# Selective-scan attention of the last layer: a new order of TensorE's work within a step, and D times u made by ScalarE

## The reference, cut to what matters

```python
u, z = jnp.split(x @ in_w.T, 2, axis=-1)
u = silu(sum(u_pad[:, k:k + L, :] * conv_w[:, k] for k in range(4)) + conv_b)
dbc = u @ xproj_w.T                                  # dt (64), B (16), C (16)
dt = softplus(dbc[..., :64] @ dt_w.T + dt_b)
dA = jnp.exp(dt[..., None] * A)
dBu = (dt * u)[..., None] * Bm[:, :, None, :]
h = dA_t * h + dBu_t ; y_t = sum_n(h * C_t)          # scan over t
y = ys.swapaxes(0, 1) + u * D
return y * silu(z) @ out_w.T
```

## Time and profile before

| | |
|---|---|
| median of 3 runs | 3783.09 us (3774.97 to 3783.92) |
| span of the profiled execution | 3806.1 us; the profile gives no other time of its own |
| stretch of the 256 scan steps | first scan 2620.0 us, last scan 3510.4 us |
| busy over the whole span | TensorE 89%, VectorE 63%, ScalarE 49%, GpSimd 45% |

### The profile page before, as it was taken

The page is one execution under the profiler, slowest core; times in us unless marked ns, Lnnn a source line. Parts: engine busy times, 40 slices in busy tenths (PEclk is TensorE's granted clock), DMA queues, the critical chain, the costliest instruction groups (busy, mean ns, idle before and its releaser), DMA issues. The chain is left out here.

```text
span 3806.1 us, 70702 instructions
## 1 busy us (share of the span) xinstructions
PE 3386.1 (89%) x24704; PEld 2274.3 (60%) x24704; DVE 2409.4 (63%) x5387; ACT 1861.9 (49%) x5051; POOL 1726.8 (45%) x1887
## 2 busy tenths in 40 slices
PE   6888888869999989999997999988999999998496
PEld 3555553547777756666663444436777777776274
DVE  3888762546666656666663444457888888888134
ACT  4666664456666635444444000036666667664033
POOL 2555541327777743333330000013676676676644
PEclk8999998989999999999998999998999999999697
DMA  4888850030000000000002777752552222222423
GB/s 132 215 210 209 210 135 11 1 76 1 2 2 2 1 1 1 2 2 1 2 1 67 159 152 152 151 101 80 122 122 71 79 78 72 79 76 65 141 69 106
DMA packets 312553, 300.58 MB, mean 79 GB/s; under 512 B 72137, under 2 KB 227721, under 8 KB 311946
## 3 DMA queue, kind: packets, MB, share of 16 engines
q1 hardware_dynamic: 307594, 286.58, 30.7%
q0 software_dynamic: 4608, 9.48, 0.8%
HBM read 237.45 MB, written 58.53 MB: 78 GB/s over the span
## 5 line engine op out<-in xcount | busy, mean ns | idle before, releaser
L2413 DVE TENSOR_TENSOR_SCAN a_h<-a_dA,a_dBu_psum 128x512 f32<-128x512 f32 x512 | 596.0, 1205 | 119.0 <-issue 106.3
L2298 POOL TENSOR_TENSOR a_h<-a_h,main_g 128x512 f32<-128x512 f32 x256 | 384.2, 1503 | 256.6 <-DVE a_h L2413 246.5
L1246 POOL TENSOR_SCALAR a_probs<-a_probs,a_row_inv 128x128 f32<-128x128 f32 (+1 forms) x512 | 381.2, 765 | 163.9 <-DVE a_row_inv L1209 163.9
L1712 DVE SCALAR_TENSOR_TENSOR m_hidden<-m_h_psum,m_gate_spread 128x512 f32<-128x512 f32 x256 | 176.9, 692 | 263.6 <-PE m_h_psum L1650 251.1
L179 POOL TENSOR_TENSOR main_g<-main_g,main_s 128x512 f32<-128x512 f32 x28 | 44.0, 1606 | 649.8 <-ACT main_g L161 649.8
L1515 POOL TENSOR_TENSOR r_position_q<-r_turned_q 128x512 f32<-128x512 f32 x128 | 160.0, 1272 | 387.3 <-DVE r_turned_q L1560 387.3
L2009 PE MATMUL a_dBu_psum<-a_B_diag,a_dt_u_turned 64*128 64x128 f32 x4096 | 317.1, 289 | 20.6 <-DVE a_h L2413 19.8
L1472 ACT ACTIVATE r_probs<-r_logits_psum,r_neg_max 128x256 f32<-128x256 f32 x512 | 235.5, 476 | 141.0 <-DVE r_neg_max L1566 141.0
L2009 PEld LDWEIGHTS a_dBu_psum<-a_B_diag,a_dt_u_turned 64*128 64x128 f32 x4096 | 257.9, 188 | 74.9 <-issue 71.0
L1151 ACT ACTIVATE a_probs<-a_logits,a_neg_max 128x128 f32<-128x128 f32 (+1 forms) x512 | 226.7, 446 | 128.3 <-DVE a_neg_max L1195 128.3
L2032 PE MATMUL a_y_psum<-main_ident,a_h 128*128 128x128 f32 x2048 | 274.8, 276 | 7.8 <-POOL a_h L2298 6.7
(11 more groups left out here) (522 smaller groups left out, 7620.3 us busy)
## 6 DMA issues: line engine op xcount, KB each, us to landing
m_gate_spread<-m_gate_rows SPq DMA_DIRECT2D x64, 1024.0 KB, 8.2
main_g<-a_b_c_rows SPq DMA_DIRECT2D x256, 256.0 KB, 3.2
a_band_rows<-main_g SPq DMA_DIRECT2D x64, 512.0 KB, 3.0
a_B<-a_band_rows SPq DMA_DIRECT2D x192, 128.0 KB, 3.3
a_A<-a_band_rows SPq DMA_DIRECT2D x192, 128.0 KB, 3.4
f_x_expert<-f_x_rows SPq DMA_DIRECT2D x16, 322.5 KB
f_x_rows<-a_zero SPq DMA_DIRECT2D x16, 320.0 KB, 5.0
f_stage_w<-L_ffn_up_weights SPq DMA_DIRECT2D x9, 512.0 KB, 6.7
```

Of the source, the lines that this page charges most:

```text
L1246: ins = nc.gpsimd.tensor_scalar(pr[:, h % NPR, tile[t]], pr[:, h % NPR, tile[t]], rinv[:, p % NST, q:q + 1], None, ALU.mult)
L2298: tt(h[:, r, :, :], h[:, r, :, :], Cs[:, g % NCS, :, :], ALU.mult).then_inc(hc_pool, 1)
L2413: nc.vector.tensor_tensor_scan(flat, dA[:, M % NDA, q, k, :, :].rearrange("p n t -> p (n t)"), db[:, 2 * (g % 2) + k, :], 0.0, ALU.mult, A ...
```

## The change

TensorE's order within a step becomes `drive(g + 1, False)`, `sum_states(g - 3)`, `drive(g + 1, True)`, then the side work; the last step's two `drive` calls are made one step early, ahead of the loop. LAG becomes 3. `u_proj` of a unit is spread: its first half moves to j = 14 and 15 of the step loop two units earlier, its second half takes one tap in each of j = 0 to 3. Both `turn_back` calls come at j = 5. D times u is made by ScalarE (`times_D`, a copy with a scale per channel), and TensorE adds it by transposes (one instruction each). ScalarE, GpSimd and VectorE get lists in a matching order.

```diff
-    LAG = 2
+    LAG = 3
-        D_diag = [s.sb(f"{x}_D_diag", [P, NK, P]) for x in DIRS]
...
-                for k in range(NK):
-                    nc.vector.tensor_scalar(dd[:, k, :], c["ident"][:], w["D"][:, k:k + 1], None, ALU.mult)
...
+                        pe.wait_ge(ud_sb, 2 * U + 2)
                         for tc in range(TC):
                             for k in range(NK):
                                 mm(yT[:, q, tc * DI + k * P:tc * DI + (k + 1) * P],
-                                   u[:, k, q * T + tc * P:q * T + (tc + 1) * P], D_diag[U % 2][:, k, :], start=tc == k == 0,
-                                   stop=False, skip_group_check=True)
+                                   ud[:, k, q * T + tc * P:q * T + (tc + 1) * P], c["ident"][:], start=tc == k == 0,
+                                   stop=False, is_transpose=True, skip_group_check=True)
...
                 drive(0, False)
+                u_proj(1, 0, (3, 2, 1, 0))
+                drive(0, True)
                 for g in range(LAST + 1):
                     U, j = g // STEPS, g % STEPS
                     N, V = U + 1, U - 1
-                    drive(g, True)
                     if g < LAST:
                         drive(g + 1, False)
+                    if g >= LAG:
+                        sum_states(g - LAG)
+                    if g < LAST:
+                        drive(g + 1, True)
+                    if U + 2 < UNITS and j in (14, 15):
+                        u_proj(U + 2, 0, ((3, 2), (1, 0))[j - 14])
                     if N < UNITS:
                         if j in (0, 1, 2, 3):
-                            u_proj(N, j // 2, ((3, 2), (1, 0))[j % 2])
+                            u_proj(N, 1, (3 - j,))
...
-                        if j in (5, 6):
-                            turn_back(V, j - 5)
+                        if j == 5:
+                            turn_back(V, 0)
+                            turn_back(V, 1)
                         if j == 10:
                             out_proj(V)
-                    if g >= LAG:
-                        sum_states(g - LAG)
...
+                def times_D(N, k):
+                    act.wait_ge(u_act, 2 * N + k + 1)
+                    if N:
                         act.wait_ge(y_mm, (N - 1) * STEPS + 2)
+                    ac(ud[:, k, :], u[:, k, :], ACT.Copy, scale=W[N % 2]["D"][:, k:k + 1]).then_inc(ud_sb, 1)
```

On ScalarE `take_turned` moves to j = 5 for both halves, `times_D` comes twice at j = 7 (and twice before the loop), `reverse` moves from j = 15 to j = 2, `take_dtu` stays at j = 13, and `decay` comes last in a step instead of near its start. On GpSimd and VectorE:

```diff
-                    if j % 2 == 0 and M < UNITS * NPAIR:
-                        spread_diagonal(M)
                     times_c(g)
+                    if j % 2 == 0 and M < UNITS * NPAIR:
+                        spread_diagonal(M)
                     if U + 1 < UNITS:
                         if j == 9:
                             add_log(U + 1, 0)
                             add_log(U + 1, 1)
-                        if j == 10:
-                            times_u(U + 1, 0)
-                            times_u(U + 1, 1)
+                        if j in (10, 11):
+                            times_u(U + 1, j - 10)
...
+                    if V >= 0 and j in (2, 3):
+                        gate(V, j - 2)
                     scan(g, 0)
                     scan(g, 1)
                     times_c(g)
-                    if V >= 0:
-                        if j in (1, 2):
-                            gate(V, j - 1)
-                        if j == 10:
-                            finish_out(V)
+                    if V >= 0 and j == 11:
+                        finish_out(V)
```

More of the change, by code:

```diff
@@ L1815, in fold_conv @@
             dve.wait_ge(weights_in, 16 * len(pairs))
-            for w, dd in zip(W, D_diag):
+            for w in W:
                 for i in range(KC):
                     nc.vector.tensor_tensor(w["conv"][:, i, :], w["conv"][:, i, :], w["in"][:, 0:DI], ALU.mult)
-                for k in range(NK):
-                    nc.vector.tensor_scalar(dd[:, k, :], c["ident"][:], w["D"][:, k:k + 1], None, ALU.mult)
         def exp_A(act, weights_in, A_exp, *_):
@@ L1862, in l3_attention @@
         tx = s.sb("x_reversed", [P, W2])
-        u = s.sb("u", [P, NK, W2])
+        u, ud = s.sb("u", [P, NK, W2]), s.sb("u_D", [P, NK, W2])
         ex = s.sb("exp", [P, NK, W2])
@@ L1882, in l3_attention @@
          dt_raw, dt_exp, dt_log, dtuT_sb, yzd_sb, dA_sb, bc_st, scanned, hc_dve, gated, summed, diag_sb, dt_sb, dtu_sb,
-         hc_pool) = s.sems(
+         hc_pool, ud_sb) = s.sems(
             "u_mm z_mm low_mm b_mm dt_mm dtuT_mm half_mm dbu_mm y_mm yzd_mm out_mm tx_sb u_act z_raw z_sb low_sb b_sb "
             "dt_raw dt_exp dt_log dtuT_sb yzd_sb dA_sb bc_st scanned hc_dve gated summed diag_sb dt_sb dtu_sb "
-            "hc_pool")
+            "hc_pool ud_sb")
         def cols(U):
@@ L2112, in silu_u @@
                     if N:
+                        act.wait_ge(dtu_sb, 2 * N)
+                        act.wait_ge(ud_sb, 2 * N)
+                    ac(u[:, k, :], pj[:, k, :], ACT.Silu, bias=W[N % 2]["cb"][:, k:k + 1]).then_inc(u_act, 1)
+                def times_D(N, k):
+                    act.wait_ge(u_act, 2 * N + k + 1)
+                    if N:
                         act.wait_ge(y_mm, (N - 1) * STEPS + 2)
-                        act.wait_ge(dtu_sb, 2 * N)
-                    ac(u[:, k, :], pj[:, k, :], ACT.Silu, bias=W[N % 2]["cb"][:, k:k + 1]).then_inc(u_act, 1)
+                    ac(ud[:, k, :], u[:, k, :], ACT.Copy, scale=W[N % 2]["D"][:, k:k + 1]).then_inc(ud_sb, 1)
                 def silu_z(U):
@@ L2200, in _ @@
                 take_dtu(0, 1)
+                times_D(0, 0)
+                times_D(0, 1)
                 for M in range(1, AHEAD):
@@ L2206, in _ @@
                     N, V = U + 1, U - 1
[L2207 to L2211, removed]
+                    if V >= 0 and j == 5:
+                        take_turned(V, 0)
+                        take_turned(V, 1)
                     if j == 4:
                         silu_z(U)
+                    if j == 2 and U % 2 and U + 2 < UNITS:
+                        reverse(U + 2)
                     if N < UNITS:
@@ L2221, in _ @@
                             take_b(N)
+                            times_D(N, 0)
+                            times_D(N, 1)
                         if j in (8, 9):
@@ L2227, in _ @@
                             take_z(N, j - 11)
[L2228 to L2231, removed]
+                        if j == 13:
+                            take_dtu(N, 0)
+                            take_dtu(N, 1)
+                    if g // 2 + AHEAD < UNITS * NPAIR:
+                        decay(g // 2 + AHEAD, j % 2)
                 take_turned(UNITS - 1, 0)
@@ L2320, in _ @@
                     M = g // 2 + 2
+                    times_c(g)
                     if j % 2 == 0 and M < UNITS * NPAIR:
                         spread_diagonal(M)
-                    times_c(g)
                     if U + 1 < UNITS:
```

## The result

The changed kernel takes 3803.26 us (median of 4 runs, 3801.15 to 3810.11) against 3780.89 for the kernel before (3774.97 to 3783.92). The ratio of the runs is on record as **1.0068**, 95% interval 1.0055 to 1.0080; the two medians alone divide to 1.0059. It is slower by 22 us between the medians. The forecast was +30 us and slower.

What follows compares the result with a forecast made beforehand. TensorE was to become the bound: a list of 56.4 us (odd) or 57.3 (even) plus a 1.6 us wait. +4 + 29 - 1.4 - 0.7 - 0.8 = +30 us gave 3813 us, range 3772 to 3842.

Steps and rivals of the forecast that it cites:

- What bounds the loop: Scan units before the change: TensorE's list 52 us of an odd unit's 56.0, so a better order wins 4 us at most.
- The seams: TensorE's switches from two-halves drives to whole-array work and back: 0.34 to 0.39 us a pair, taken as 0.36.
- How many seams: Every TensorE step with side work gets two pairs, only j = 4 not: 15 more pairs, +5.4 us a unit.
- The chain: From dt_proj through add_log and GpSimd's times_u to turn_dtu at j = 13: TensorE waits 1.6 us a unit, lost in full.
- No chain wait: Rival: ScalarE and GpSimd run earlier, the 1.6 us fall away in 15 units, -24, so 3789 us; chance 0.18.
- the third rival: GpSimd's block at j = 9 to 12 makes sum_states and the drive wait: 1.5 us a unit more, 3836 us; chance 0.13.
- One sign: VectorE's waits in the scans should go to the drives, spread over nearly all steps; no size given.
- The two rules weighed there: TensorE's new seams: hidden by early weight loads (list 51.0 us; rival 3757 us, chance 0.13), or paid by draining (56.4 us).
- The start: Four taps before the first second-drive at 1.2 GHz: +5 us before the first scan, +4 in all with unit 0.
- The sum: Whole kernel: +4 start, +29 units 1 to 14, -1.4 unit 14, -0.7 last unit, -0.8 D diagonals: +30 us.

Runs made afterwards that it cites:

- The last kernel: The kernel with three waits taken out, with GpSimd's diagonal of B ahead of times_c, and at j = 10 diagonal, times_u twice, times_c: 3724.14 us.
- the kernel with three waits taken out: Kernel with the old step order, plus both times_u at j = 9, finish_out before j = 11's scans, taps behind first second-drive: 3755.00 us.

## Why the prediction was right, point by point

- **What bounds the loop.** Right. I added TensorE's list up to 52 us of 56.0 and said that a better order could win the 4 us of idle at most, beside D times u. The last kernel has that list, less 0.9, with one seam pair a step, which is 51.0 us for an odd and 51.9 for an even unit by the prediction's sum. It takes 52.17 and 53.13. Of the 1.2 us that the sum lacks, 0.7 lies in three rows of 16 drive instructions that last 1.43, 1.49 and 1.25 instead of 1.16. One reason given beside it was wrong: that in the new order the side work "no longer stands before the scans' release". It still stands between one release and the next.
- **The seams.** Right in kind and price. The price is 0.35 us a pair, read from steps without a wait (3.37 against 3.02). That it decides the time is shown by undoing the order (39 us) and by adding the second pair alone to that kernel (37 us).
- **How many seams.** This is the term that was mis-sized: "Only j = 4 has none, so 15 more pairs come to a unit". It is 13. `dt_proj` uses 64 rows and starts at the first row, and the drive's instructions mix with it without a seam; the `dt_proj` steps take 2.97 us in both orders. The 2 x 0.36 = 0.7 us a unit are more than the difference between 58.0 and 57.39. The wait was 0.25 shorter besides, so some 0.35 us a unit were missing elsewhere in the sum; where is not shown. The trace of the kernel before had it. TensorE's timeline there:

```profile
3046.03 1.16 PE L2009 MATMUL a_dBu_psum<-a_B_diag,a_dt_u_turned 64*128 64x128 f32 x16
3047.03 1.02 PE L1956 MATMUL a_pj_psum<-a_dt_B_C,a_f_dt 64*128 64x512 f32 x2
3047.98 1.09 PE L2032 MATMUL a_y_psum<-main_ident,a_h 128*128 128x128 f32 x8
3049.00 1.16 PE L2009 MATMUL a_dBu_psum<-a_B_diag,a_dt_u_turned 64*128 64x128 f32 x16
```

  The next row starts 1.00 us after the drives, where transposes start 1.09 after them, and the transposes behind `dt_proj` take 1.02, as behind a drive, not the 0.97 that they take behind whole-array work. I took it for a seam between `drive` and side work; it lies between `dt_proj` and `sum_states`.
- **The chain.** Right: "It waits 1.6 us", measured 1.35. The chain from `dt_proj` to the first `add_log` took 5.96 us (3065.65 to 3071.61; forecast 5.95). Without the wait the kernel gained 24 us, as the rival *No chain wait* had it; that kernel stands at 0.9997. GpSimd's block did not make `sum_states` wait, so the third rival did not happen. One sign came only in part: VectorE waited for drives in 118 of the 219 steps between 2700 and 3490, not in nearly all.
- **The two rules weighed there.** The Trainium skill, TensorE: Matmul & The Clock Gate, Part 3, has weight loads pulled ahead; by that the new seams would be hidden. The trace of the changed kernel does not agree: 0.75 us beyond the paces in a step with two seam pairs. The Trainium skill, TensorEngine Tiling (Array Packing), "Key Properties", has a change of mode drain TensorE; the 0.35 us of a pair agree with that.
- **The start.** "+5 us before the first scan" was near. The first scan came 9.2 us later; `fold_conv`, ahead of the part that changes, began 3.3 us later in that execution (2556.57 instead of 2553.28), so 6 are the start's. Unit 0 won back only 0.25 of it (55.27 instead of 55.52). So the start was a little dearer than the +4 of the sum; moving the taps gained 7 us by the medians and 2.6 by the trace.
- **The sum.** Units 1 to 14 brought +20 us, not +28 (29 less 1.4); the start about +6, not +4, units 0 and 15 together -0.7; in all about +25 by the trace, +22 by the medians, +30 forecast. That the total came so near is due in part to errors that go against each other: two pairs of seams too many, a start and some rest of each unit too low.

The part of the change that is shown to be a gain is D times u by ScalarE: 16 us, alone. The evened steps, the moved lists and LAG 3 together are not: with all of them and the old order the kernel takes 3764.43 us, with D times u alone 3764.91. Their stretch is 6 us shorter (870.6 against 876.9), but it begins 6.6 us later (2625.2 against 2618.7), behind the four taps. The order that gave the change its name cost 39 us, more than twice the gain.

## What to carry to other kernels

If an engine is busy for nine tenths of a loop, add its list up before changing its order: an order that feeds the consumer earlier is worth at most the idle time, and here it lengthened the list. On TensorE count how often the list goes from matmuls on parts of the rows to whole-array ones and back, and keep the parts together. When a wait is taken out, ask on the releasing engine what now stands behind the instruction that was moved up: one kernel here traded a wait for `dt*u` (1.33 us) for one of about the same size for a diagonal (1.55).

## What the runs showed of the hardware that was not expected

- A change from the two-halves mode to the whole array and back costs 0.35 us (one-tap steps of 3.02 us with one pair; 3.37 and 3.36 with two, in two kernels), with the granted clock at 1.00 in the middle of the stretch (2700 to 3490 in the changed kernel).
- Matmuls of 64 rows at the first row of the array (`dt_proj`) go together with two-halves matmuls without that cost: the first pair of the next drive starts at 3065.66, between the two `dt_proj` instructions at 3065.65 and 3066.08.
- A drive that must wait for the end of the one just before it loses 0.36 us (1.52 against 1.16 for 16 instructions). In this kernel a pair of seams and such a wait cost the same, so to trade one for the other wins nothing.
- In the kernel with three waits taken out, TensorE idles about 1.55 us for the diagonal in every middle unit. In two of them the granted clock then read 0.50 for 3.3 us, and these units took 1.6 us more (55.51 against 53.90).
